# Two attention layers of a gated cross-attention stack: the rows of the operand stacks interleaved over the partitions

## What is computed

```
x = x + tanh(g_xattn[0]) * cross_attention_0(ln(x), ctx)        # softmax over the queries
x = x + tanh(g_ffn[0])   * routed_low_rank_ffn(ln(x))           # 6 experts, 100 landmarks
x = x + tanh(g_xattn[1]) * cross_attention_1(ctx, ctx, ln(x))   # 16 heads of 16 channels
x = x + tanh(g_ffn[1])   * self_attention(ln(x))                # 16 heads of 16 channels
# cross_attention_1 and self_attention, per head of D = 16 channels:
energy = einsum('bqhd,bkhd->bhqk', q, k)
out    = einsum('bhqk,bkhd->bqhd', softmax(energy / 4), v)
# self_attention takes 1024 keys, a key mask by the class of a token, and 5 register tokens apart
```

## Time and profile before

| | |
|---|---|
| Median of 3 runs | 1269.52 us (1268.82 to 1273.41) |
| Profiled execution, its own time | 1271.61 us |
| Its span in the profile | 1269.8 us |
| PE busy | 1190.4 us, 94% |
| DVE busy | 972.3 us, 77% |
| ACT busy | 818.0 us, 64% |
| POOL busy | 258.2 us, 20% |
| DMA packets of the hardware queue | 89872, 100.06 MB, 39.1% of 16 engines |

### The profile page before, as it was taken

The page is one execution under the profiler, slowest core; times in us unless marked ns, Lnnn a source line. Parts: engine busy times, 40 slices in busy tenths (PEclk is TensorE's granted clock), DMA queues, the critical chain, the costliest instruction groups (busy, mean ns, idle before and its releaser), DMA issues.

```text
span 1269.8 us, 26173 instructions
## 1 busy us (share of the span) xinstructions
PE 1190.4 (94%) x10392; PEld 546.1 (43%) x10392; DVE 972.3 (77%) x1431; ACT 818.0 (64%) x1471; POOL 258.2 (20%) x200
## 2 busy tenths in 40 slices
PE   4888998999999899988999999999999999999997
PEld 2566685555558456443232322332232323332345
DVE  4896477665537749568999999999999999999902
ACT  1324465677752653214888888888888888888871
POOL 2130343555651332460000000000000000000000
PEclk9879998899999999998999999999999999999999
DMA  6100217556500234444335552554436543454014
GB/s 198 27 1 1 38 36 156 95 108 128 90 27 1 99 125 137 114 55 66 65 68 100 75 98 64 97 99 68 95 67 101 92 83 79 85 97 78 11 49 130
DMA packets 89993, 101.73 MB, mean 80 GB/s; under 512 B 22154, under 2 KB 60300, under 8 KB 89872
## 3 DMA queue, kind: packets, MB, share of 16 engines
q1 hardware_dynamic: 89872, 100.06, 39.1%
HBM read 71.47 MB, written 24.33 MB: 75 GB/s over the span
## 4 chain that ended last, share of the span: by engine, by line
PE 58%; DVE 33%; ACT 3%; issue 2%; SPq 1%; DMA 1%; POOL 0%; POOLq 0%; DVEq 0%; ACTq 0%
DVE sm L2217 23%; PE ps L1687 10%; PE ps L1678 9%; PE ps L1665 7%; PE ps L1453 3%; PE ps L1548 2%; PE ps L1444 2%; PE ps L1445 2%; PE ps L1748 2%; PE ps L1507 2%; PE ps L1462 1%; PE ps L1411 1%; PE ps L1409 1%; DVE XN L1825 1%; PE ps L1568 1%
## 5 line engine op out<-in xcount | busy, mean ns | idle before, releaser
L2217 DVE TENSOR_REDUCE sm<-ps 128x1 f32<-128x1024 f32 x512 | 602.0, 1219 | 33.9 <-PE ps L1665 29.8
L1152 ACT ACTIVATE W<-ps 128x512 f32<-128x512 f32 x1024 | 535.0, 604 | 123.3 <-PE ps L1687 120.9
L1687 PE MATMUL ps<-R 99*32 99x512 bf16 x4096 | 317.5, 384 | 0.9
L1678 PE MATMUL ps<-W,R 128*32 128x512 f32 x2048 | 265.3, 594 | 0.0
L1687 PEld LDWEIGHTS ps<-R 99*32 99x32 bf16 x4096 | 85.2, 94 | 203.5 <-ACT W L1152 156.3
L1665 PE MATMUL ps<-R 50*128 50x512 bf16 x512 | 90.9, 390 | 12.7 <-DVE sm L2217 8.3
L1665 PE MATMUL ps<-KM,R 50*128 50x512 bf16 x512 | 88.7, 384 | 5.2 <-DVE sm L2217 0.2
L1075 ACT ACTIVATE R<-ps 77x512 f32<-77x512 f32 x128 | 75.1, 592 | 28.1 <-PE ps L1445 19.0
L901 POOL COPY R<-R 128x512 f32<-128x512 f32 x16 | 9.7, 611 | 385.1 <-PE ps L1678 385.1
L1678 PEld LDWEIGHTS ps<-W,R 128*32 128x32 f32 x2048 | 62.9, 111 | 45.8 <-issue 0.5
L831 POOL COPY R<-R 4x2048 bf16<-4x2048 bf16 x32 | 60.5, 1890 | 66.0 <-ACT R L1055 56.1
(11 more groups left out here) (259 smaller groups left out, 1504.6 us busy)
## 6 DMA issues: line engine op xcount, KB each, us to landing
R<-x_parts SPq DMA_DIRECT2D x96, 128.0 KB, 4.9
R<-q_parts SPq DMA_DIRECT2D x192, 64.0 KB
R<-q_parts SPq DMA_DIRECT2D x96, 128.0 KB
R<-k_parts SPq DMA_DIRECT2D x96, 128.0 KB
q_parts<-R SPq DMA_DIRECT2D x24, 256.0 KB, 2.6
k_parts<-R SPq DMA_DIRECT2D x24, 256.0 KB, 2.7
x_parts<-R SPq DMA_DIRECT2D x6, 768.0 KB, 6.1
X<-in_x SPq DMA_DIRECT2D x4, 1024.0 KB, 9.7
```

Source lines behind the costliest of these rows:

```text
L1152: act.activation(PR[:, s % 2, h, :], third_bank("score", 64 * u + n), ACT.Exp, scale=0.25).then_inc(s_sfree, 1)
L1678: mm = pe.matmul(bank(7)[32 * h:32 * h + 32, :], VST[j][:, k, h, :], PR[:, s % 2, h, :], start=(k == 0), stop=(k == TB - 1))
L1687: mm = pe.matmul(o[32 * c:32 * c + 32, :], KST[j][0:MAX_ROW + 1, h, t:t + 32], QST[j][0:MAX_ROW + 1, h, 512 * (s // 8):512 * (s // 8) + 51 ...
L2217: dve.tensor_reduce(MX[:, half, h, q:q + 1], bank(2 * ((p + 1) % 2), 2), AX, ALU.max).then_inc(s_tfree, 1)
```

## The change

Each of the five loads puts its 16 rows at every sixth partition (stacks of six blocks) or every third (stacks of three) and not side by side: block n of a stack takes the partitions n, n+6, n+12, ... n+90, or n, n+3, ... n+45. Row of part-block n and channel d moves from partition 16n + d to 6d + n (or 3d + n). Number, size, order and source of the DMAs are as before, the extra rows from 96 (or 48) are where they were, and every engine, SP too, has the same instructions in the same order.

```
-                sp.dma_start(K1s[16 * n:16 * n + 16],
+                sp.dma_start(K1s[n:SR:6],
                              KXP[p].rearrange("(h d) n -> d h n", d=D)).then_inc(s_k1s, 16)
...
-                    sp.dma_start(Xs[u % 3][16 * n:16 * n + 16],
+                    sp.dma_start(Xs[u % 3][n:SR:6],
                                  XP[p, 64 * hg:64 * hg + 64, S * b:S * b + S]
                                  .rearrange("(j d) t -> d j t", d=D)).then_inc(s_xs[u % 3], 16)
...
-                        sp.dma_start(dst[16 * n:16 * n + 16], src[u]).then_inc(s_stk[j], 16)
+                        sp.dma_start(dst[n:SR:6], src[u]).then_inc(s_stk[j], 16)
...
-                            sp.dma_start(QMP[j][g][64 * t + 16 * n:64 * t + 16 * n + 16]
+                            sp.dma_start(QMP[j][g][64 * t + n:64 * t + CLS_ROW:3]
                                          .rearrange("p (j n) -> p j n", j=2), src[u][g]).then_inc(s_mst[j], 16)
...
-                        sp.dma_start(KM[j][64 * t + 16 * n:64 * t + 16 * n + 16], src[u][t]).then_inc(s_mst[j], 16)
+                        sp.dma_start(KM[j][64 * t + n:64 * t + CLS_ROW:3], src[u][t]).then_inc(s_mst[j], 16)
```

## The result

The median after is 1275.56 us (12 runs, 1271.02 to 1278.32), before 1270.21 us (12 runs beside them, 1266.93 to 1273.90). The ratio is 1.0033 with a 95% interval of 1.0018 to 1.0048, some 4 us slower (2.3 to 6.1). That is within 0.5%, as forecast, but a real loss and outside the range, which ended at 1273.5. One run of full_only (1494.4 us at a granted clock of 0.745) was disturbed and is left out of its ratio, but not of its median.

What follows compares the result with a forecast made beforehand. TensorE and VectorE were taken to bound the kernel, with DMAs holding 1% of the chain. All terms were 0 us, giving 1271.61 us profiled or 1269.5 us as median; the eight-in-ten range was 1266.0 to 1273.5 us.

Steps and rivals of the forecast that it cites:

- Loads get faster: All changed stack loads: spread rows land sooner, about 2 us gained per stack, from 7.9 us in unit 3.
- Xs, K1s and the full stacks at 0 us: Cross-attention and self-attention loads: all land before TensorE's first use, so faster landing moves nothing, 0 us.
- The faster rival: Cross-attention's start: late loads cause the stalls there, so 11 us would be regained, 1258.5 us; chance 0.05.
- the slower one: Ahead of line 1409: spread rows load more slowly, 66 us at twice the time, 1335 us; chance 0.04.
- No instruction is added, removed or moved: All 582 changed DMAs: only where their rows land changes; no size was given for SP's issuing.
- both bounds of a stack: Six Xs loads: 5.3 us near, 11.2 us far, each a landing time behind SP's 2.2 us of issuing.
- nothing in the rows points to a cost per partition step: Xs loads ahead of line 1409: argument against spread rows loading more slowly; no size of its own.
- What shares the queue ... 0 us: SP's queue, row of maxima and projections' key-part write: faster loads shorten waits there, but nothing is gained, 0 us.
- could start earlier: Projections: ScalarE's 2.97 us wait for key parts could shorten, but VectorE is busy until 504.59, so 0 us.
- about 3.7 us: Self-attention: time from SP's issue at 746.00 to the row of maxima's first user, the score matmul at 749.75.
- The maximum stacks' spare time: Self-attention, QMP and KM: loads have landed over 5 us before TensorE turns to them behind 632.63, so 0 us.
- Within 0.5%: Whole kernel: time stays within 6.3 us, about what a measurement can tell from no change; chance 0.91.

Runs made afterwards that it cites:

- full_only: Only the self-attention's full stacks (QST, KST) interleaved, against the kernel before: 1271.02 us, ratio 0.9989.
- cross_only: Only the cross-attention's loads (K1s, Xs) interleaved, against the kernel before: 1271.52 us, ratio 1.0015.
- cross_full: K1s, Xs, QST and KST interleaved, all but the stacks for the maxima, against the kernel before: 1270.00 us, ratio 1.0007.
- more_loads: The kernel before, rows side by side, with each QMP load of line 613 cut into two of half the size: 1302.34 us, ratio 1.0267.
- rest_row: The changed kernel with the first eighteen maximum-stack loads side by side again and the row of maxima stored earlier: 1270.18 us, 1.0004 against before.

## Why the prediction was right or wrong

- **Loads get faster: right.** I took 2 us per stack; unit 3 gained 1.8 us or a little more (7.9 to at most 6.1). Between 716 and 720 us the DMA engines move 195 GB/s at a share of 0.66, where it was 139 at 1.12. All of it was hidden, as the rows had said.
- **Xs, K1s and the full stacks at 0 us: right**, within the intervals of cross_only, full_only and cross_full. The faster rival and the slower one, loads that hold TensorE up at line 1409, both fell.
- **"No instruction is added, removed or moved", so no cost of issuing: this step failed.** The sum has no term for SP's time per issue; it is put at nothing without a reason. The text took the 2.2 us that SP needs for six issues into both bounds of a stack, as if it could not change, and bounded only the landing; it also held that "nothing in the rows points to a cost per partition step". The instruction was the same, its duration was not: 595 ns in place of 426.
- **"What shares the queue ... 0 us": failed with it, at both places.** Of line 1123 I wrote that ScalarE "could start earlier", and asked only what a gain would be worth. The rows held the answer to the other question: with 0.35 us between the end of ScalarE's copy (504.24) and VectorE's need (504.59), any delay of that write beyond 0.35 us goes straight on. 3.1 us more came: 2.4 us in stage B. The row of maxima was given "about 3.7 us" from issue to use; that is issue, flight and spare together (the row landed 1.8 us before its use), and at the tightest row the spare was gone: 0.9 us in stage D. The store of that row was said to stand "behind stack loads" and to gain from faster ones. SP's waits between lines 669 and 671 did shrink, from 90.3 to 50.1 us between 620 and 1200 us, but not for the rows that are tight: those stand behind line 705.
- **Both bounds were too near for this reason.** A row for a slower issue was in the trace of before, though not among those read: line 686, another form of load on the same queue, takes 589 ns. With it as the far bound, 18 x (589 - 426) = 2.9 us, less 0.35 of cover, gives 2.6 us for the projections, which would have moved the range's upper end to about 1276.
- **The maximum stacks' spare time: right, from the wrong line.** The row at 632.63 is a score matmul, which does not read them; the maximum tiles turn to the new stack at 634.47.
- **Within 0.5%: right by luck.** The price that the sum left out happened to be small; with SP's time raised in more_loads, which interleaves nothing, the same two places cost 2.7%.

No kernel of the study is shown to be faster than the kernel before. rest_row, cross_full and full_only stand level with before, their intervals holding 1: where no one waits for the loads, the spread buys nothing even when it costs nothing.

## What to carry to other kernels

A DMA has two prices, the time on the queue that issues it and the time until it lands, and an edit to its access pattern can make one better and the other worse. Before changing loads, list what stands behind them in the issuing queue and read how much cover each of those has; a wait with 0.3 us of cover passes on whatever the queue adds. And where a trace shows a wait that "could end earlier", ask what a later end would cost, since the cover on the two sides is seldom the same.

## What the runs showed of the hardware

- SP's issue of a load from DRAM to 16 partitions takes 423 to 426 ns (median) with neighbouring partitions and 592 to 596 ns with a step of 2, 3 or 6, for 64 KB and for 128 KB alike; for the 154 KB of line 538 it is 448 and 609 ns. Why is open.
- The same 96 loads of 128 KB land after 3.0 us (median) in place of 4.9, at longest 4.5 in place of 9.0, and the queue's share of 16 engines falls from 39.1% to 26.8% at equal bytes.
- In the executions profiled, kernels with the same work up to the projections reach them between 458.7 and 465.8 us, and the low clock falls in different places. With one profile each, differences of a few microseconds are to be read stage by stage, and only where several kernels agree.
